# The next block's first set of two sparse neighbour sums is joined ahead of the block's last fetch

## The reference

```python
x = _layernorm(x + _L2_gnn_ref(x, edge_index, edge_weight1, ...))   # convolution
x = _layernorm(x + _L3_gnn_ref(x, edge_index, edge_weight, ...))    # weighted sum
...
    norm = dinv[src] * dinv[dst]
    h = x @ W
    msg = h[src] * norm[:, None]
    agg = jax.ops.segment_sum(msg, dst, num_segments=n) + b
...
    msg = edge_weight[:, None] * x[src]
    agg = jax.ops.segment_sum(msg, dst, num_segments=N)
    out = (1.0 + EPS) * x + agg
```

## Time and profile before

| | us |
|---|---|
| median of 3 runs | 11548.42 |
| lowest and highest of them | 11541.08, 11550.59 |
| the profiled execution | 11562.99 |
| its span | 11561.4 |

### The profile page before, as it was taken

One profiled execution on the slowest core, in us unless ns is written; L12 is line 12 of the kernel. 1 busy time (PEld: TensorE's weight loads), 2 busy tenths in 40 slices (PEclk: granted clock), 3 DMA queues, 4 the chain that ended last, 5 costly groups with the idle time before them and its releaser, 6 DMA issues. The chain is left out here.

```text
span 11561.4 us, 331562 instructions
## 1 busy us (share of the span) xinstructions
PE 8920.2 (77%) x101102; PEld 7210.5 (62%) x101103; DVE 8515.2 (74%) x17511; ACT 4614.1 (40%) x9076; POOL 1655.6 (14%) x2115
## 2 busy tenths in 40 slices
PE   6144557885888755899994888798899959849996
PEld 5132224664777644899993655433899946649995
DVE  7497777777999866666666666666788867788887
ACT  0021001112666411566663333476677746613332
POOL 0010000110000000466661000000000003301110
PEclk9999999998999855999997999899999979979996
DMA  1100000000444311333333999677455510000000
GB/s 37 13 0 11 4 4 8 11 11 12 168 165 165 124 36 31 112 123 125 125 123 103 320 313 322 229 250 237 131 144 144 144 40 5 5 3 3 3 3 12
DMA packets 617056, 1103.62 MB, mean 95 GB/s; under 512 B 119640, under 2 KB 207539, under 8 KB 616992
## 3 DMA queue, kind: packets, MB, share of 16 engines
q1 hardware_dynamic: 487488, 923.21, 25.3%
q10 hardware_dynamic: 121152, 168.86, 3.9%
q0 software_dynamic: 8352, 10.85, 0.4%
HBM read 901.57 MB, written 201.10 MB: 95 GB/s over the span
## 5 line engine op out<-in xcount | busy, mean ns | idle before, releaser
L2439 POOL TENSOR_TENSOR acc<-acc,m_sum 128x544 f32<-128x544 f32 (+1 forms) x637 | 816.2, 1281 | 1237.5 <-ACT m_sum L2406 953.6
L2369 PE MATMUL m_sps<-m_msg,m_oh 128*128 128x136 f32 x5096 | 722.5, 286 | 0.0
L2304 DVE TENSOR_TENSOR m_msg<-m_vps,m_msg 128x512 f32<-128x512 f32 x637 | 440.7, 692 | 361.4 <-PE m_vps L2345 269.9
L2558 DVE BATCH_NORM_STATS2 stats<-t_es 128x512 f32 x637 | 442.2, 694 | 353.0 <-ACT t_es L2591 351.6
L2759 PE MATMUL u_sps<-u_r,u_oh 128*128 128x128 f32 x5096 | 678.1, 276 | 28.7 <-ACT u_r L2717 28.7
L2570 PE MATMUL t_eps<-t_oht,p_parts 128*128 128x512 bf16 x1911 | 527.9, 386 | 211.8 <-DVE t_oht L1472 208.3
L2743 PE MATMUL u_zps<-fcs,u_a 128*128 128x128 f32 x5112 | 677.5, 276 | 7.3 <-ACT u_a L2711 7.3
L2644 PE MATMUL g_z<-g_a,fcT 128*128 128x512 f32 x1274 | 616.2, 616 | 66.2 <-ACT g_a L2633 54.4
L1408 PE MATMUL sp_out_x<-x,sp_adj_x 128*128 128x128 f32 x4802 | 661.8, 281 | 0.0
L1392 PE MATMUL sp_aps_x<-sp_ohw_x,sp_oh_x 128*128 128x128 bf16 x7644 | 545.2, 219 | 146.6 <-DVE sp_ohw_x L1359 146.6
L1421 ACT COPY sp_adj_x<-sp_aps_x 128x512 f32<-128x512 f32 x637 | 373.4, 586 | 702.4 <-PE sp_aps_x L1392 702.4
(11 more groups left out here) (584 smaller groups left out, 21493.9 us busy)
## 6 DMA issues: line engine op xcount, KB each, us to landing
u_e<-e_tiles SPq DMA_DIRECT2D x640, 256.0 KB, 2.8
e_tiles<-t_es ACTq DMA_DIRECT2D x637, 256.0 KB, 5.6
g_e<-e_tiles SPq DMA_DIRECT2D x637, 256.0 KB, 3.5
s_rows<-bucket_rows SPq DMA_DIRECT2D x148, 768.0 KB, 4.0
m_rows<-bucket_rows SPq DMA_DIRECT2D x148, 768.0 KB, 4.1
t_rows<-bucket_rows SPq DMA_DIRECT2D x148, 768.0 KB, 7.1
s_rows<-bucket_rows SPq DMA_DIRECT2D x49, 1024.0 KB, 5.3
m_rows<-bucket_rows SPq DMA_DIRECT2D x49, 1024.0 KB, 5.3
```

The costliest lines, as they stand in the source:

```text
L2369: last = nc.tensor.matmul(sps[x][:, at:at + M], oh[x][:, j * P:(j + 1) * P], msg[x][:, j * M:(j + 1) * M], start=True, stop=True)
L2439: nc.gpsimd.tensor_tensor(at, at, sums[x][:, 0:n * M], ALU.add).then_inc(added, 1)
```

## The change

In `phase_spmm`, and so in both passes:

- The ring gets a fifth place. As 13 sets over 4 places leave a rest of 1, set 12 has it for itself, and sets 0 to 11 go round the four.
- PE's steps become functions `join(w, q)` and `fetch(w, q)`. Join 0 of the first block stands ahead of the loop. In the loop each fetch q follows join q+1, and for q = 12 that is join 0 of the next block: join 12, fetch 11, join 0 (next), fetch 12, then join 1 of the next block.
- ACT's copies are moved in the same way: the copy of set 0 of the next block comes after that of set 12 and ahead of the total.
- DVE is moved on by one set: pair q+2 and weigh q+1 stand in the place of pair q+1 and weigh q, over the block's edge. Each pair now has the wait for the list.
- After the last block the steps of a block that doesn't exist follow: two pairs, a product (in the weighted pass), a join and a copy of set 0. SP loads one list more for them (`again`), once DVE has freed a half.
- POOL's wait ahead of the overflow rows names set 12's own place.
- In the caller the buffer `h_rest` (25.6 KB in each partition) is released before the first pass.

```diff
-def load_lists(nc, B, sp, lst, nw, lists_free, lists_go, lists_in, lists_ready):
+def load_lists(nc, B, sp, lst, nw, lists_free, lists_go, lists_in, lists_ready, again=False):
...
+    if again:
+        sp.wait_ge(lists_free, nw + 1)
+        sp.sem_inc(lists_go, 1)
+        sp.dma_start(lst[:, bass.ds((nw & 1) * B.cols, B.cols)], B.lists[0:P, :]).then_inc(lists_in, 16)
+        sp.wait_ge(lists_in, nw * 16 + 16)
+        sp.sem_inc(lists_ready, 1)
...
-    R = Ring(NQ, 4)
+    R = Ring(NQ, 4, True)
...
-                load_lists(nc, B, sp, lst, B.windows(sp, s), lists_free, lists_go, lists_in, lists_ready)
+                load_lists(nc, B, sp, lst, B.windows(sp, s), lists_free, lists_go, lists_in, lists_ready, True)
...
-                with dve.Fori(0, nw) as w:
+
+                def pair(w, q):
+                    r = R.slot(q)
                     at = (w & 1) * B.cols
                     dve.wait_ge(lists_ready, w + 1)
-
-                    def pair(q):
+                    dve.wait_ge(adj_made[r], R.before(w, q) + 1)
+                    pair_one_hot(nc, k, oh[r], lst, at + q * FG).then_inc(paired[r] if weighted else oh_made[r], 1)
+
+                def weigh(w, q):
                         r = R.slot(q)
-                        dve.wait_ge(adj_made[r], R.before(w, q) + 1)
-                        pair_one_hot(nc, k, oh[r], lst, at + q * FG).then_inc(paired[r] if weighted else oh_made[r], 1)
-
-                    def weigh(q):
-                        r = R.slot(q)
+                        at = (w & 1) * B.cols
                         dve.wait_ge(paired[r], R.before(w, q) + 1)
...
-                    pair(0)
+                pair(0, 0)
+                pair(0, 1)
+                if weighted:
+                    weigh(0, 0)
+                with dve.Fori(0, nw) as w:
                     for q in range(NQ):
-                        if q + 1 < NQ:
-                            pair(q + 1)
+                        pair(w + (q + 2) // NQ, (q + 2) % NQ)
                         if weighted:
-                            weigh(q)
+                            weigh(w + (q + 1) // NQ, (q + 1) % NQ)
 
                     dve.wait_ge(oh_made[R.slot(last_q)], R.before(w, last_q) + 1)
                     dve.sem_inc(lists_free, 1)
...
+                def join(w, q):
+                    r = R.slot(q)
+                    pe.wait_ge(oh_made[r], R.before(w, q) + 1)
+                    pe.wait_ge(adj_copied[r], R.before(w, q) + 1)
...
+                def fetch(w, p):
+                    r = R.slot(p)
+                    pe.wait_ge(adj_copied[r], R.before(w, p) + 2)
+                    if p == 0:
+                        pe.wait_ge(gathered, w + 1)
+                    if p == last_q:
+                        pe.wait_ge(over_set, w + 1)
...
+                join(0, 0)
                 with pe.Fori(0, nw) as w:
-                    for q in range(NQ + 1):
-                        if q < NQ:
-                            r = R.slot(q)
-                            pe.wait_ge(oh_made[r], R.before(w, q) + 1)
-                            pe.wait_ge(adj_copied[r], R.before(w, q) + 1)
...
-                        if q >= 1:
-                            p = q - 1
-                            r = R.slot(p)
-                            pe.wait_ge(adj_copied[r], R.before(w, p) + 2)
-                            if p == 0:
-                                pe.wait_ge(gathered, w + 1)
-                            if p == last_q:
-                                pe.wait_ge(over_set, w + 1)
...
+                    for q in range(NQ):
+                        join(w + (q + 1) // NQ, (q + 1) % NQ)
+                        fetch(w, q)
...
+                def take(w, q):
+                    r = R.slot(q)
+                    act.wait_ge(adj_made[r], R.before(w, q) + 2)
+                    act.wait_ge(used[r], R.before(w, q) + 1)
+                    nc.scalar.copy(adj[r][:, :], aps[r][:, :]).then_inc(adj_copied[r], 1)
+                take(0, 0)
                 with act.Fori(0, nw) as w:
                     for q in range(NQ):
-                        r = R.slot(q)
-                        act.wait_ge(adj_made[r], R.before(w, q) + 2)
-                        act.wait_ge(used[r], R.before(w, q) + 1)
-                        nc.scalar.copy(adj[r][:, :], aps[r][:, :]).then_inc(adj_copied[r], 1)
+                        take(w + (q + 1) // NQ, (q + 1) % NQ)
                     r = R.slot(last_q)
                     act.wait_ge(used[r], R.before(w, last_q) + 2)
                     act.wait_ge(total_free, w + 1)
...
-                    pool.wait_ge(used[r], R.before(w, 0) + 1)
+                    pool.wait_ge(used[r], R.done(w, r) + 1)
...
-                h3, hr = tile(c1, "h_parts", 3 * NF, BF16), tile(c1, "h_rest", NF)
-                phase_parts(nc, s, k, h, hr, h3)
+                h3 = tile(c1, "h_parts", 3 * NF, BF16)
+                with ExitStack() as c2:
+                    phase_parts(nc, s, k, h, tile(c2, "h_rest", NF), h3)
                 phase_spmm(nc, s, k, B, h3, 3 * D, acc, False, "_g")
```

More of the change, by code:

```diff
@@ L1379, in _ @@
                     pe.sem_inc(used[r], 1)
-                with pe.Fori(0, nw) as w:
-                    for q in range(NQ + 1):
-                        if q < NQ:
-                            r = R.slot(q)
-                            pe.wait_ge(oh_made[r], R.before(w, q) + 1)
-                            pe.wait_ge(adj_copied[r], R.before(w, q) + 1)
-                            for t in range(G):
-                                part = aps[r][:, t * P:(t + 1) * P]
-                                at_src = of_pair(oh[r][:, :], P, t)
-                                if weighted:
-                                    w5 = ohw[r][:, :].rearrange("p (q c v t) -> p q c v t", q=2, c=3, t=2)
-                                    for c in range(3):
-                                        last = nc.tensor.matmul(part, at_src, w5[:, t // 2, c, :, t % 2], start=(c == 0), stop=(c == 2))
-                                else:
-                                    last = nc.tensor.matmul(part, at_src, of_pair(oh[r][:, :], P, G + t), start=True, stop=True)
-                            last.then_inc(adj_made[r], 1)
-                        if q >= 1:
-                            p = q - 1
-                            r = R.slot(p)
-                            pe.wait_ge(adj_copied[r], R.before(w, p) + 2)
-                            if p == 0:
-                                pe.wait_ge(gathered, w + 1)
-                            if p == last_q:
-                                pe.wait_ge(over_set, w + 1)
-                            for t in range(G):
-                                tile = p * G + t
-                                rhs = table[:, tile * width:(tile + 1) * width] if tile < s.NB else \
-                                    over[:, (tile - s.NB) * width:(tile - s.NB + 1) * width]
-                                last = nc.tensor.matmul(out[:, :], adj[r][:, t * P:(t + 1) * P], rhs, start=(tile == 0), stop=(tile == NT - 1))
-                            last.then_inc(used[r], 1)
@@ new lines, in join @@
+                def join(w, q):
+                    r = R.slot(q)
+                    pe.wait_ge(oh_made[r], R.before(w, q) + 1)
+                    pe.wait_ge(adj_copied[r], R.before(w, q) + 1)
+                    for t in range(G):
+                        part = aps[r][:, t * P:(t + 1) * P]
+                        at_src = of_pair(oh[r][:, :], P, t)
+                        if weighted:
+                            w5 = ohw[r][:, :].rearrange("p (q c v t) -> p q c v t", q=2, c=3, t=2)
+                            for c in range(3):
+                                last = nc.tensor.matmul(part, at_src, w5[:, t // 2, c, :, t % 2], start=(c == 0), stop=(c == 2))
+                        else:
+                            last = nc.tensor.matmul(part, at_src, of_pair(oh[r][:, :], P, G + t), start=True, stop=True)
+                    last.then_inc(adj_made[r], 1)
@@ new lines, in fetch @@
+                def fetch(w, p):
[5 more added lines that the diff above has]
+                        pe.wait_ge(over_set, w + 1)
+                    for t in range(G):
+                        tile = p * G + t
+                        rhs = table[:, tile * width:(tile + 1) * width] if tile < s.NB else \
+                            over[:, (tile - s.NB) * width:(tile - s.NB + 1) * width]
+                        last = nc.tensor.matmul(out[:, :], adj[r][:, t * P:(t + 1) * P], rhs, start=(tile == 0), stop=(tile == NT - 1))
+                    last.then_inc(used[r], 1)
```

## The result

| | before | after |
|---|---|---|
| median, us | 11544.75 | 11431.51 |
| lowest and highest, us | 11535.7, 11550.59 | 11424.78, 11434.97 |
| span of the profiled execution, us | 11561.4 | 11433.2 |
| pass `_g`, to the start of its last total, us | 617.6 | 590.0 |
| pass `_x`, to the start of its last total, us | 1127.8 | 1043.6 |

After over before is 0.9902 (95% interval 0.989 to 0.9915), four runs of each. The medians differ by 113.2 us, and the two passes of the profiled executions by 27.6 + 84.2 = 111.8. The interval allows anything from 98 to 127 us, so that the two figures lie this close is in part luck.

The account below looks back on a forecast made before the run. PE was taken as the bound, busy 94% of both passes, idling at block boundaries for DVE (`_x`) and an ACT copy (`_g`). 84.7 + 27.8 - 0.7 = 111.8 us off 11548.4 gave 11436.6 us, range 11422 to 11462.

Parts of the forecast that it names:

- The sum: Whole kernel: 84.7 + 27.8 - 0.7 = 111.8 us gained, 11436.6 us; this forecast had chance 0.80.
- The first pass: `_g`, block boundary: fetch 0 comes 0.58 us earlier, times 48 boundaries 27.8 us gained.
- The stall that stays: `_g`, block boundary: PE still idles about 0.4 to 0.6 us a block, waiting for the total.
- The second pass: `_x`: 1.78 us a boundary vanishes, times 48 is 85.4 us; less 0.71 us for an extra join, 84.7 gained.
- The hand-over rival: `_x`: a stall of 0.3 to 0.6 us a block stays, 14 to 29 us less gain, about 11458; chance 0.12.
- the cover: `_x`, boundary: the total is out and handed over at 10833.41, fetch 0 due at 10833.55, covered by 0.14 us only.
- The clears: End of each pass: POOL clears five more semaphores; ten more cost between 0 and 1.4 us, taken as 0.7.
- the whole 1.78 us of a boundary in `_x`: `_x`: from fetch 0 to the next block's is 23.01 us where 13 steps are 21.23; the boundary shrinks to nothing.
- DVE's slack: `_x`: DVE needs 19.75 us for a block's 13 sets against PE's 21.23, 1.4 us spare.
- What is late next is DVE's throughput: `_x`, after the fifth place: DVE's 19.75 us a block would be the next limit, staying under PE's 21.23.
- The rivals of a slower kernel: Both passes: loop bodies leave the instruction store, 11668 us by two fetches a block, or the clock falls; chance 0.04 together.
- The clock: Both passes: a fuller PE might run at half rate, 7% of some 1630 us eating the gain; counted within 0.04.

Follow-up runs that it names:

- e1: The kernel before with the fifth ring place alone, order of all steps untouched: `_x` 1060.8 us, median 11483.49 us, ratio 0.9947 to before.
- e4: The whole change in the weighted pass `_x` alone, `_g` made by the function of before: `_x` 1044.3 us, median 11469.95 us, ratio 0.9931.
- e5: The changed kernel with two output banks that alternate by block: `_g` 579.4 us, median 11426.41 us, ratio 0.9891 to before.
- e3: The whole change in the unweighted pass `_g` alone, `_x` made by the function of before: `_g` 590.6 us, median 11522.73 us, ratio 0.998.
- e7: The changed kernel with one more unread product a block on DVE in `_x` (set 6): `_x` 1044.4 us, median 11446.09 us, ratio 0.9912.
- e11: The changed kernel with GpSimd's addition of a block's total cut from 128 columns to 2: `_x` 1043.9 us, median 11443.49 us, ratio 0.9898.
- e12_dve_3_copy: The changed kernel with three more products a block on DVE in `_x` and GpSimd's addition replaced by a copy: `_x` 1267.6 us, median 11672.51 us.
- e8_dve_3: The changed kernel with three more unread products a block on DVE in `_x` (sets 3, 6, 9): `_x` 1274.7 us, median 11678.51 us, ratio 1.0113.

## Why the prediction was right

**The sum.** 11437 us was predicted, 11431.5 measured, 0.05% less and within 11422 to 11462. The gain of 113.2 us between the medians stands against 111.8. That the total fits to a tenth of a per cent is in part luck: the parts below are each off by up to half a microsecond, and 10 us behind `_x` that nobody predicted lie within what the medians can't tell.

**The first pass.** Predicted 27.8, measured 27.6 in the windows. Fetch 12 to fetch 0 was to be 9801.88 - 9800.42 = 1.46 us and is 1.39, but fetch 12 doesn't start as before: behind join 0 it comes 0.08 us later, and the two cancel. The stall that stays is named rightly, the total, if a little long (0.34 us of idle PE, 0.4 to 0.6 predicted); the run with two banks shows that it is the bank, but also that freeing it gives back only 11 of the 24 us that 1.39 - 0.88 held.

**The second pass.** Predicted 84.7, measured 84.2: no wait of PE, a step of 1.63 us, 12 matmuls more. The hand-over rival (0.12) fell, but its ground was sound: the cover was reckoned at 0.14 us and is 0.17 by the same reckoning (10799.61 - 10799.39 - 0.05 for the hand-over), and the run with the total behind copy 1 lost 53 us. Moving the total back by one copy would have made that rival and more.

**The clears.** From the start of `_x`'s last total to DVE's first instruction of the next stage it was 11388.58 - 11384.51 = 4.07 us and is 11270.64 - 11266.25 = 4.39: 0.32 us for five clears more (4.39 too in the three other runs with the fifth place that were read, e1, e4 and e5; 4.07 in e3, where `_x` has four places). Behind `_g` the same stretch went from 10108.80 - 10103.11 = 5.69 to 10075.21 - 10069.21 = 6.00 us. Together 0.63, where 0.7 was taken. `_g` clears five arrays too, not four.

**Which part does what.** The prediction gave the whole 1.78 us of a boundary in `_x` to both edits together and didn't split it. The place alone brings 67 us and the order 17; in `_g` the order without the place loses 20 us and the place without the order gives 0.7.

**DVE's slack: the mis-sized step.** The prediction had 1.4 us spare a block and DVE stopped by the ring several times, about 1.5 us in sum. It is stopped once, for 0.8 us, and the rest of its time is small gaps. The slack by work is larger than I read (a set takes 1.47 us, not 19.75 / 13 = 1.52, which makes 21.23 - 19.11 = 2.1 us a block), and the slack that counts is smaller: one product hides, two, 1.74 us, lose 86.6 us, where by a slack of 1.4 they would have lost (1.74 - 1.4) x 48 = 16, because what the idle time of DVE pays for is GpSimd's turn. The forecast didn't hang on it, as nothing is added to DVE in the change; but the sentence "What is late next is DVE's throughput" named the wrong engine.

**The rivals of a slower kernel.** The two instruction queues moved 3 packets in `_x` as before: the DMA view of after has

```profile
q8 instruction: 2, 0.03, 0.0%
q14 instruction: 1, 0.01, 0.0%
```

so the loops stay loaded, and the waits views give PEld next to no idle time without a releaser: 1.1 us in the whole of `_g`, none in `_x`. The clock stayed at 1.00 with PE 100% busy for 1044 us.

**Not predicted.** The profiled spans differ by 128.2 us, 16.4 more than the passes give. 6.3 of it lies ahead of `_g` (9485.5 to 9479.2), where the work is the same and the other runs began that pass at 9462 to 9500, so that is the spread between runs. 9.9 lies behind `_x`: between 11342 and 11382 us of the kernel after the granted clock is 0.88, a stretch at the upper level in a stage that runs at 0.50 ahead of it and behind it, while the windows view of before has, in the same stage,

```profile
11470.00:11510.00 40.00, 25.90 (x94) 19.59 (x94) 27.00 (x94) 9.90 (x32) 0.00 (x0) 0.50 0.00 0
```

0.50, the lower level (1.2 GHz), as nearly everywhere in that stage. The stage took 167 to 172 us in the kernels in which both passes have the new order and PE never idles in `_x` (after, e5, e7, e11) and 177 to 179 in all others, those with one pass changed and those in which PE waits in `_x` among them. Each of the four has one such stretch at 0.9 to 1.00 (in e7 it comes earlier in the stage), none of the others has. Why it differs stays open: what the clock depends on was not tested, and there is one trace of each kernel. If the 9.9 us belong to the change, it is worth some 122 us, which the medians (98 to 127) allow as well as 111.8.

## What to carry over

Where a ring's size divides badly into the number of sets, look at the boundary: a place of its own for the last set lets the producer run over it, and only then can the consumer's order be moved over it too. What hands over the one shared output bank goes right behind the last step that writes it and ahead of every copy that isn't needed yet; here one copy in front of it would have cost 53 of the 84 us. And don't fill VectorE's last idle microsecond from its busy sum: ask what GpSimd has to do in that time, and who waits for that.

## What the runs showed of the hardware

- GpSimd's operation took as long as VectorE's two-input instructions followed each other without a gap: 23.3 us for an addition that takes 0.5, 23.05 for one of two columns, 23.16 for a copy, ending 0.06 to 0.3 us after VectorE's last one. The profile books the wait as busy time of GpSimd (618 us of POOL in `_x` of e12_dve_3_copy, 99 us in the kernel after), so a POOL that looks busy may be waiting.
- VectorE's records overlap by 0.07 to 0.08 us when it runs back to back, so the durations of a set, 0.68 + 0.94 = 1.62 us, overstate what it needs, 1.47 us.
- The first weight load of a block's fetch 0 idled 0.3 us with no releaser in the profile, with an output address from a register (e5_two_banks, `_g`) and with a fixed one (e1_ring_only, `_x`).
- While PE idled 7.4 us in e8_dve_3 its granted clock fell from 1.00 to 0.50, and for some 3 us after it matmuls ran at that level. In `_x` of that run, at a mean clock of 0.93, PE was busy 51.6 us longer than in the kernel after, on top of 179.5 us of waiting.
